# Experts' weights with neighbouring rows in one partition, read back with strides

## What is computed

```python
logits = einsum('bsd,de->bse', x, gate_w) + gate_b        # 16 experts
top_probs, top_idx = top_k(softmax(logits), 2)            # two experts per node
h1 = einsum('bsd,edh->bseh', x, w1)                       # 256 -> 512
h2 = einsum('bsd,edh->bseh', x, w2)                       # 256 -> 512
hidden = silu(h1) * h2
expert_out = einsum('bseh,eho->bseo', hidden, w3)         # 512 -> 256
out = sum over the two experts, weighted by top_probs
```

## Time and profile before

| | |
|---|---|
| Time, median of 3 runs | 2617.94 us (2611.76 to 2624.79) |
| The profiled execution's own time | 2628.59 us |
| Its span | 2626.8 us |
| Busy in the span: TensorE matmul, weight load | 1950.6 us (74%), 1716.4 us (65%) |
| VectorE, ScalarE, GpSimd | 1404.9 (53%), 1095.4 (42%), 1649.3 us (63%) |
| First to last `hidden` of the experts' blocks | starts at 1449.79 and 1805.67 us |

### The profile page before, as it was taken

The page is one execution under the profiler, slowest core; times in us unless marked ns, Lnnn a source line. Parts: engine busy times, 40 slices in busy tenths (PEclk is TensorE's granted clock), DMA queues, the critical chain, the costliest instruction groups (busy, mean ns, idle before and its releaser), DMA issues. The chain is left out here.

```text
span 2626.8 us, 42480 instructions
## 1 busy us (share of the span) xinstructions
PE 1950.6 (74%) x12455; PEld 1716.4 (65%) x12456; DVE 1404.9 (53%) x4132; ACT 1095.4 (42%) x2065; POOL 1649.3 (63%) x1454
## 2 busy tenths in 40 slices
PE   2499999999999999993931888885246666661878
PEld 2488887888888888883830787774234444441866
DVE  5376676666766665662625111112665555556874
ACT  1266555565556555552310111110146666652321
POOL 1278887788877877776646777772457777770000
PEclk9799999999999999996955999998678878785988
DMA  6566665666666666666011788885233333362001
GB/s 162 143 130 136 136 131 119 120 138 135 127 131 136 130 127 136 130 118 119 2 40 31 250 280 275 271 269 178 72 100 105 105 104 105 105 94 38 1 10 39
DMA packets 196527, 326.78 MB, mean 124 GB/s; under 512 B 37800, under 2 KB 119309, under 8 KB 195720
## 3 DMA queue, kind: packets, MB, share of 16 engines
q0 software_dynamic: 92320, 142.07, 27.6%
q1 hardware_dynamic: 103250, 182.55, 23.6%
q10 hardware_dynamic: 900, 1.50, 0.3%
HBM read 261.01 MB, written 64.99 MB: 124 GB/s over the span
## 5 line engine op out<-in xcount | busy, mean ns | idle before, releaser
L665 POOL DMA_INDIRECT edge_sums<-edge_agg,edge_slot x316 | 540.2, 1709 | 154.4 <-issue 80.8
L656 POOL DMA_INDIRECT edge_nf<-node_table,edge_node_idx x316 | 342.5, 1084 | 174.4 <-issue 85.3
L1768 POOL DMA_INDIRECT att_got<-head_table,att_idx x352 | 336.7, 956 | 125.2 <-issue 85.1
L494 PE MATMUL edge_e_ps<-edge_w_high,edge_hid_low 128*128 128x256 f32 x1264 | 370.6, 293 | 48.0 <-DVE edge_pre L861 38.4
L1001 POOL DMA_INDIRECT slot_table<-by_src_pair,by_src_row_i x320 | 312.2, 975 | 111.7 <-issue 95.4
L856 DVE TENSOR_TENSOR edge_hid_low<-edge_whole,edge_hid_high 128x512 fp32r<-128x512 f32 x316 | 214.5, 690 | 308.2 <-ACT edge_hid_high L798 307.5
L495 PE MATMUL edge_e_ps<-edge_w_low,edge_hid_high 128*128 128x256 f32 x1264 | 354.7, 281 | 0.0
L496 PE MATMUL edge_e_ps<-edge_w_high,edge_hid_high 128*128 128x256 f32 x1264 | 354.5, 280 | 0.0
L494 PEld LDWEIGHTS edge_e_ps<-edge_w_high,edge_hid_low 128*128 128x128 f32 x1264 | 242.1, 191 | 71.8 <-DVE edge_pre L861 49.0
L494 PE MATMUL edge_h_ps<-edge_eat_high,edge_w_low 128*128 128x512 f32 x632 | 252.1, 399 | 24.4 <-DVE edge_eat_low L852 23.6
L1802 PE MATMUL att_s_ps<-att_w,att_hot 128*125 128x258 f32 x704 | 243.4, 506 | 8.8 <-DVE att_hot L1880 5.7
(11 more groups left out here) (338 smaller groups left out, 3760.9 us busy)
## 6 DMA issues: line engine op xcount, KB each, us to landing
moe_w<-in_L_ffn_w_dram SPq DMA_DIRECT2D x162, 512.0 KB
edge_ea<-in_edge_attr_dram SPq DMA_DIRECT2D x77, 448.0 KB
edge_dst_row<-dst_rows SPq DMA_DIRECT2D x79, 256.0 KB, 4.6
routed<-moe_out SPq DMA_DIRECT2D x54, 128.0 KB
att_got<-head_table,att_idx POOLq DMA_INDIRECT x352
slot_table<-by_src_pair,by_src_row_i POOLq DMA_INDIRECT x320
edge_nf<-node_table,edge_node_idx POOLq DMA_INDIRECT x316
edge_sums<-edge_agg,edge_slot POOLq DMA_INDIRECT x316
```

Of the source, the lines that this page charges most:

```text
L494: pe.matmul(out, ll, rh, start=start, stop=False)
L656: pool.indirect_dma_start(nf[u][:, j, :], None, m.node_table[:, :], bass.IndirectOffsetOnAxis(ap=node_idx[u][:, j:j + 1], axis=0)).then_in ...
L665: pool.indirect_dma_start(m.sums[k][:, :], bass.IndirectOffsetOnAxis(ap=slot[u][:, j:j + 1], axis=0), agg[u][:, j, :], None, compute_op=AL ...
L1768: pool.indirect_dma_start(got[v][:, j, :], None, m.head_table[:, :], bass.IndirectOffsetOnAxis(ap=idx[v][:, j:j + 1], axis=0)).then_inc(la ...
```

## The change

The three weights are laid so that a partition holds rows that are neighbours in memory. Partition p now holds rows 2p and 2p + 1 of w1 and w2 (one run of 4 KB), and rows 4p to 4p + 3 of w3 (one run of 4 KB). Products add over these rows, so the other operand must be laid the same way. The node rows are therefore turned with a step of two numbers (8 bytes): half k of the turned rows holds features k, 2 + k, 4 + k and so on. And chunk c of the hidden numbers must hold the numbers c, 4 + c, 8 + c and so on, so `hidden` reads the columns of w1 and w2 with a step of four numbers (16 bytes). The shapes, the number of instructions, the buffers and the waits are as before.

```diff
@@ moe_experts, load (SP)
-                        sp.dma_start(w[:], wd[one, :, :].rearrange("a (k p) h -> p (a k) h", p=P)).then_inc(w_in[u], 16)
+                        sp.dma_start(w[:], wd[one, :, :].rearrange("a (p k) h -> p (a k) h", p=P)).then_inc(w_in[u], 16)
@@ transposes (TensorE)
-                        last = nc.tensor.transpose(t_ps[:, kd, 0:P], rows[u][:, kd * P:(kd + 1) * P], m.ident[:])
+                        last = nc.tensor.transpose(t_ps[:, kd, 0:P], rows[u][:].rearrange("p (d k) -> p k d", k=KD)[:, kd, :], m.ident[:])
@@ hidden (TensorE)
-                                last = nc.tensor.matmul(h_ps[:, c, :], w[:, kd, c * P:(c + 1) * P], xt[u][:, kd, :],
+                                last = nc.tensor.matmul(h_ps[:, c, :], w[:, kd, :].rearrange("p (h c) -> p c h", c=KH)[:, c, :], xt[u][:, kd, :],
```

## The result

The changed kernel takes 2767.05 us (median of 4 runs, 2756.82 to 2773.43) against 2621.36 us for the kernel before beside it: the ratio is 1.0558, with a 95% interval of 1.0514 to 1.0603. The profiled execution took 2767.18 us, its span is 2765.4 us.

The account below looks back on a forecast made before the run. Waits between weight loads and `rows_out` were taken to bound blocks; slower `hidden` loads would make TensorE bound: +102.6 us over 53 blocks, +3.1 last block, +2 first, together +108 on 2618, so 2726 us; likeliest case 2696 to 2756, range 2600 to 2756.

Parts of the forecast that it names:

- What bounds a block: Experts' stage: 6.71 us a block, set by waits, above floors of TensorE alone, 5.52 us, and GpSimd alone, 6.36 us.
- the round of waits: Experts' blocks: weight issue waits for `rows_out` to free a buffer, `hidden` waits for the weights; 7.36 us from issue to use.
- The signs forecast for the profile: `hidden`'s 32 loads near 6.8 us, its 49.5 us weight wait near nothing, GpSimd waiting longer, q1 near 25 bytes per ns.
- Nothing of the DMAs' gain arrives once `hidden` is slow: Weight DMAs: 0.35 us a block saved by 4 KB packets buys nothing, hidden behind TensorE's loop of 8.65 us.
- The column step: `hidden`'s weight loads, columns 16 bytes apart: 114 ns becomes 212 ns (194 to 228), 3.13 us more a block.
- The node rows: Two loads a block in `transposes`, 8 bytes apart: taken as nothing, at most 0.23 us a block, 12 us for the range.
- The first block's slow clock: First block's `hidden` loads run at the lower clock, 6.35 us instead of 3.65 before the change: +2 us.
- The rival that the stride is free: `hidden`'s strided loads stay hidden beside the matmul, only the DMA saving remains: 2609 us (2600 to 2618), chance 0.38.
- The clock: Rival: in the experts' stage the granted clock falls as the array idles between loads, giving 2842 us; chance 0.04.

Follow-up runs that it names:

- the two with the split wait: Kernel before, w1 and w2 loads issued after `hidden`, not `rows_out`, of three blocks earlier: 2590.67 us; same with w1, w2 in 4 KB runs: 2595.07 us.

## Why the prediction was wrong

- *What bounds a block* was right: the round of waits, with TensorE's floor of 5.52 us and GpSimd's of 6.36 us below it. The kernel before and the two with the split wait show all three. The signs forecast for the profile came as said, but for the size of the load and the pace of the queue.
- *Nothing of the DMAs' gain arrives once `hidden` is slow* was right: 2760.55 us with the step alone against 2767.05 us with all three edits. The gain of a transfer was sized at 0.35 us a block and measured 0.28 with the long runs alone. The pace itself was taken too high: 25 bytes per ns were forecast for queue q1 after the change, and 43.30 MB in 52.2% of 16 engines over 240 us are 21.6.
- *The column step* failed in its size, the term that carried the sum. I took VectorE's ratio of paces, 1.86, on the 114 ns of a load: 212 ns, at most 228. Measured: 235.6 ns, 3.89 us a block instead of 3.13, and 53 x 0.76 = 40 us of the miss: the change costs 2767.05 - 2621.36 = 145.7 us where +108 was forecast. The measured 2767 us lies above the range's end of 2756, which was no bound but the same conversion with a sum in place of a ratio. What stood wrong is the conversion: it put a ratio, or an addition, on the 114 ns that a load of neighbouring numbers takes. What fits the runs is a time per number taken from its own place. VectorE's 1.93 ns read so, 128 x 1.93 = 247 ns, was in the rows and I did not use it as an end; the runs give 1.84 ns on TensorE. That VectorE's figure has the same cause is not shown: no run varies its step.
- *The node rows* were taken as free, and were. Their loads did go from 143 to 197 ns (145 with the step in the columns alone), but `hidden` starts 0.33 us behind the first of them either way, and TensorE's loop is 9.41 us by the columns alone, so nothing of it reaches the block.
- *The first block's slow clock* was given 2 us. It cost nothing to speak of: 7.57 us for that `hidden`, 0.03 more than any other. And with no `rows_out` between them the first two `hidden` are 7.71 us apart, not 9.41. These two take back 3.7 us of the 40.
- *The rival that the stride is free* took the shorter loads of `transposes` as slack. The slack is real, but small: at 8 bytes a load takes 120 ns of the stream against 114, at 12 bytes 177. That the matmul beside the load sets the 114 ns is the reading that fits; no run here changes the matmul alone.
- *The clock* did not fall: the granted clock is 1.00 in the stretch shown, in which TensorE has no gap.

The rule that two reads of a 16 byte line are needed, from the Trainium skill's Advanced Engine Details and Errata, section SBUF Cachelines, fits `hidden` here: two numbers a line cost 6 ns a load, one costs 122. It does not fit the transposes' loads, which take 143 ns with four numbers a line and 197 with two; there the measurement decides.

## What to carry to other kernels

A step in a float32 operand of TensorE has a price that can be estimated before: count the pieces of 16 bytes that the numbers lie in, times 1.8 ns, and compare with what the instruction takes of the stream now. In these runs only what went beyond that was paid, so 8 bytes between numbers are nearly free and 16 bytes double both the load and the moving side. Types other than float32 were not run. And before transfers are made faster, look for what gates their issue: an earlier wait gained 1.0% where longer runs of all three weights, in a kernel that does not compute the reference, gained 0.5%; the longer runs that could be kept, of w1 and w2, gained nothing that could be measured, with or without the earlier wait.

## What the runs showed of the hardware that was not expected

A strided load does not get slower when the granted clock falls. In the changed kernel's first block, busy times by stretch show the clock at 0.50 of full speed, the level of 1.2 GHz, after TensorE had stood nearly idle (0.32 of 3 us), and further on 1.00, the level of 2.4:

```profile
1438.00:1441.00 3.00, 0.32 (x2) 0.35 (x3) 0.00 (x0) 0.00 (x0) 2.39 (x3) 0.50 0.99 379
1441.00:1443.00 2.00, 2.00 (x11) 2.00 (x9) 0.42 (x1) 0.00 (x0) 1.39 (x3) 0.50 1.00 396
...
1445.00:1447.00 2.00, 2.00 (x10) 2.00 (x9) 0.00 (x0) 0.59 (x1) 1.39 (x3) 1.00 0.04 9
```

The group of its weight loads in 1441 to 1443.5 us:

```profile
L1451 PEld LDWEIGHTS moe_h_ps<-moe_xt,moe_w 128*128 128x128 f32 x11 | 2.7, 330 | 0.0
```

330 ns at half the clock, 328 over all 1728 loads; a load of neighbouring numbers takes 333 ns at half the clock in the kernel before (1449.8 to 1453 us) and 194 over its stage. Whole blocks say the same: the first `hidden`, partly at half the clock, takes 7.57 us against 7.54 with the step, and 6.35 against 3.65 without. So the pace of the pieces, 1.84 ns, does not follow the gated clock. Nor does it follow the DMA traffic: the DMA engines are busy for 1.00 of the first stretch with loads and 0.04 of the last. That the pace is the memory's is a reading that no run here tests further.
